# Graph network on one core: types counted by turn in the second permutation and in the pair counts, ranking by maximum, one register table, first gathers beside the table

## What is computed

```python
seg = concatenate([edge_type * n + src, (edge_type + R) * n + dst])   # R = 9, n = 3125
srcs = concatenate([dst, src])
# per layer: every node's row times 18 weight matrices; each edge takes the row of
# its far end and its type, scaled by factors of the counts of seg; sums by near end
deg = segment_sum(ones, dst, n)
```

## Time and profile before

| What | Value |
|---|---|
| Median of three runs | 5796.72 us |
| The profiled execution | 5791.65 us |
| Its span, first to last instruction | 5790.0 us |
| Busy: TensorE products, VectorE, GpSimd, ScalarE | 4358.3, 2903.5, 2059.3, 1183.2 us |
| Mean granted TensorE clock | 0.756 |
| First ranking and its permutation | about 15 to 411 us |
| Second ranking and its permutation | about 424 to 832 us |
| Staircase, pair counts | 874 to 896, 896 to 1325 us |
| Rgcn layer 0: table, sums | 3242 to 3340, 3345 to 4395 us |
| Rgcn layer 1: table, sums | 4420 to 4518, 4522 to about 5560 us |

### The profile page before, as it was taken

One profiled execution on the slowest core, in us unless ns is written; L12 is line 12 of the kernel. 1 busy time (PEld: TensorE's weight loads), 2 busy tenths in 40 slices (PEclk: granted clock), 3 DMA queues, 4 the chain that ended last, 5 costly groups with the idle time before them and its releaser, 6 DMA issues. The chain is left out here.

```text
span 5790.0 us, 73260 instructions
## 1 busy us (share of the span) xinstructions
PE 4358.3 (75%) x16465; PEld 2333.0 (40%) x16467; DVE 2903.5 (50%) x7206; ACT 1183.2 (20%) x3146; POOL 2059.3 (36%) x2143
## 2 busy tenths in 40 slices
PE   4985985557999996999978767767777666566658
PEld 1221221113655552454434355555553333343434
DVE  8999997761188886101152744433444422222233
ACT  3974973441400003111121100000000000000001
POOL 0000001110067760000000067777772577777730
PEclk9997996668999998999989855555557655555569
DMA  0000001225188881525514422222225322322233
GB/s 15 0 0 0 0 0 68 102 102 179 64 283 292 297 269 66 176 86 176 175 42 142 189 79 53 53 53 53 53 53 163 112 53 53 53 53 53 53 64 113
DMA packets 155477, 562.58 MB, mean 97 GB/s; under 512 B 42865, under 2 KB 51410, under 8 KB 155101
## 3 DMA queue, kind: packets, MB, share of 16 engines
q0 software_dynamic: 86816, 274.40, 16.9%
q1 hardware_dynamic: 68150, 286.11, 13.7%
q10 hardware_dynamic: 390, 0.60, 0.0%
HBM read 449.10 MB, written 111.85 MB: 97 GB/s over the span
## 5 line engine op out<-in xcount | busy, mean ns | idle before, releaser
L1850 PE MATMUL ps_sum_rgcn<-select_sum_rgcn,gathered_sum_rgcn 128*128 128x128 f32 x3328 | 1273.8, 492 | 564.4 <-DMA gathered_sum_rgcn<-by_dst,row 272.3
L1773 POOL DMA_INDIRECT gathered_sum_rgcn<-by_src,row x832 | 785.0, 944 | 1523.5 <-SPq L1734 1270.6
L1850 PEld LDWEIGHTS ps_sum_rgcn<-select_sum_rgcn,gathered_sum_rgcn 128*128 128x128 f32 x3328 | 839.3, 314 | 874.5 <-issue 866.6
L1773 POOL DMA_INDIRECT gathered_sum_rgcn<-by_dst,row x832 | 790.5, 950 | 253.5 <-issue 205.7
L608 PE MATMUL ps_sum_arma<-gathered_sum_arma,select_sum_arma 128*128 128x384 f32 x1664 | 554.0, 492 | 18.0 <-DMA gathered_sum_arma<-arma,other 15.4
L1459 PE MATMUL ps_sum_arma<-pair_counts_sum_arma,parts_sum_arma 128*128 128x512 f16 x2625 | 539.1, 361 | 14.2 <-DVE outT_arma_mid L1994 5.6
L594 POOL DMA_INDIRECT gathered_sum_arma<-arma,other x416 | 393.3, 945 | 435.7 <-POOLq L680 269.2
L1919 DVE TENSOR_TENSOR select_sum_rgcn<-one_hot_sum_rgcn,ps_coef_sum_rgcn 128x2048 f32<-128x2048 bf16 x52 | 118.9, 2287 | 769.1 <-PE ps_sum_rgcn L1850 769.1
L1880 ACT COPY sums_sum_rgcn<-ps_sum_rgcn 128x128 f32<-128x128 f32 x100 | 26.5, 265 | 2094.7 <-PE ps_sum_rgcn L1850 2094.7
L642 DVE TENSOR_TENSOR acc_arma_end<-acc_arma_end,ps_sum_arma 128x768 f32 x416 | 396.9, 954 | 57.1 <-PE ps_sum_arma L608 35.3
L608 PEld LDWEIGHTS ps_sum_arma<-gathered_sum_arma,select_sum_arma 128*128 128x128 f32 x1664 | 307.6, 190 | 264.2 <-issue 63.2
(11 more groups left out here) (385 smaller groups left out, 5765.2 us busy)
## 6 DMA issues: line engine op xcount, KB each, us to landing
pair_counts_sum_arma<-pairs SPq DMA_DIRECT2D x125, 800.0 KB, 4.3
by_src<-rows_rgcn_table SPq DMA_DIRECT2D x50, 576.0 KB, 2.8
by_dst<-rows_rgcn_table SPq DMA_DIRECT2D x50, 576.0 KB, 3.7
exact<-whole_pairs SPq DMA_DIRECT2D x25, 800.0 KB, 3.3
pairs<-half_pairs SPq DMA_DIRECT2D x25, 800.0 KB, 3.3
pair_counts_sum_x<-pairs SPq DMA_DIRECT2D x25, 800.0 KB, 4.4
pair_counts_sum_gcn<-pairs SPq DMA_DIRECT2D x25, 800.0 KB, 4.3
air_counts_sum_neighbour<-pairs SPq DMA_DIRECT2D x25, 800.0 KB, 4.3
```

The lines of the kernel that those rows point to most:

```text
L1773: nc.gpsimd.indirect_dma_start(got[:, n % PLACES, :], None, table, bass.IndirectOffsetOnAxis(ap=o.row[:, n % C:n % C + 1], axis=0)).then_i ...
L1850: nc.tensor.matmul(ps[:, bass.ds(ring[2 * v], P)], got[:, p, :], select[:, parity, u, :], start=False, stop=False, skip_group_check=True). ...
```

## The change

- `rank_stage`: TensorE sums the columns of all tiles so that a tile lies in a partition (`spot` picks the row). VectorE scans 400 (416) totals at once and computes a base per tile and column. For each of 25 blocks TensorE adds four products in PSUM (rank in the column, a large constant where the edge belongs to the tile, and the base in two bf16 parts), and VectorE takes the maximum over the blocks in two running buffers. ScalarE's copies of totals go.
- `Permute`: the group one-hot goes. High half and place come from one VectorE operation (compare, then multiply, with two scalars per partition); ScalarE makes the low half alone. Only the second permutation (by source, from the list by destination) counts, and it counts by destination: per turn of 16 columns VectorE makes type one-hots 9 wide, TensorE loads 16 group numbers of the chunks into registers and adds a product of nine columns at the group's place.
- Pair counts: the counts by source are made here, nine columns for each of the first 416 items, with type one-hots of all chunks made first. Four tables become two: TensorE loads one table of four values an item (place, column, free, group), VectorE one of two.
- Rgcn: the table stage is split in two of nine types (pieces of three, 384 columns). GpSimd's queue issues the first 32 gathers beside the second; the gathered buffer is now held by `rgcn_layer`.
- The second sort stands ahead of the degree stage; heavy and factor stages stand after the pair counts.

```diff
-            dve.wait_ge(kept, B + BLOCKS)
+            dve.wait_ge(totaled, 1)
+            then(nc.vector.tensor_copy(total[:, :], ps[0:NT, 0, 0:W]))
             then(nc.vector.tensor_tensor_scan(upto[:, :], total[:, :], total[:, :], 0.0, ALU.add, ALU.max))
...
+            for b in range(NT):
+                dve.wait_ge(filled_in, b + 1)
+                if b >= 2:
+                    dve.wait_ge(higher, b - 1)
+                nc.vector.tensor_tensor(best[e, b % 2, :], best[e, b % 2, :], ps[e, 3 + b % B, 0:W],
+                                        ALU.max).then_inc(higher, 1)
...
+                nc.tensor.matmul(place, triangle[0:ROWS, 0:ROWS], one_hot[0:ROWS, b, :], start=True, stop=False)
+                nc.tensor.matmul(place, big[0:ROWS, 0:ROWS], one_hot[0:ROWS, b, :], start=False, stop=False)
+                if b == 0:
+                    pe.wait_ge(shown, 1)
+                for part in (0, 1):
+                    last = nc.tensor.matmul(place, row_of[:, b, 0:ROWS], parts[:, part, :], start=False, stop=(part == 1))
+                last.then_inc(filled_in, 1)
...
+        if self.counts and u == 0:
+            dve.wait_ge(self.moved, i * U + self.V)
+            nc.vector.tensor_tensor(self.type[:, :, :], l.type[:, bass.ds(i * U, U), None].to_broadcast([P, U, R]),
+                                    k.iota[:, None, 0:R].to_broadcast([P, U, R]), ALU.is_equal).then_inc(self.typed, 1)
         dve.wait_ge(self.moved, n + 1)
         nc.vector.tensor_scalar(self.place[e, v, :], k.iota16[e, 0:P], o.slot_in[e, col], None,
                                 ALU.is_equal).then_inc(self.placed, 1)
-        nc.vector.tensor_scalar(self.chunk[e, v, :], k.iota16[e, 0:C], o.chunk_in[e, col], None, ALU.is_equal)
-        nc.vector.tensor_scalar(self.local[e, v, :], k.iota16[e, 0:P], o.local_in[e, col], None, ALU.is_equal)
-        nc.vector.tensor_scalar(self.group[e, v, :], k.iota16[e, 0:self.G], o.group_in[e, col], None,
+        nc.vector.tensor_scalar(self.slot[e, v, 0, :], k.iota16[e, 0:P], o.slot_in[e, col], o.high_in[e, col],
+                                ALU.is_equal, ALU.mult)
+        if self.counts:
+            nc.vector.tensor_scalar(self.local[e, v, :], k.iota16[e, 0:P], l.local[e, col], None, ALU.is_equal)
+        nc.vector.tensor_scalar(self.chunk[e, v, :], k.iota16[e, 0:C], o.chunk_in[e, col], None,
                                 ALU.is_equal).then_inc(self.column, 1)
...
+            nc.vector.tensor_tensor(type_hot[:, :, :], o.type[:, :, None].to_broadcast([P, C, R]),
+                                    k.iota[:, None, 0:R].to_broadcast([P, C, R]), ALU.is_equal)
...
-                places = load(PE, q.held_at, i * V, V, HELD - 1)
-                columns = load(PE, q.column_at, i * V, V, (SPANS - 1) * SPAN)
-                free = load(PE, q.free_at, i * V, V, BLOCKS_OF_PAIRS)
+                table = load(PE, q.item_at, i * (4 * V), 4 * V, (SPANS - 1) * SPAN)
                 for u in range(V):
-                    pe.wait_ge(freed, free[u])
+                    place, column, free, group = (
+                        nc.s_assert_within(x, low, top, skip_runtime_bounds_check_because="the staircase stays within its blocks")
+                        for x, low, top in zip(table[4 * u:4 * u + 4], (0, 0, 1, 0),
+                                               (HELD - 1, (SPANS - 1) * SPAN, BLOCKS_OF_PAIRS, G - R)))
                     pe.wait_ge(made, i * V + u + 1)
+                    if more:
+                        nc.tensor.matmul(ps_count[:, bass.ds(group, R)],
+                                         source[:, bass.ds(i * V + (u - base), 1), :].rearrange("p a f -> p (a f)"),
+                                         type_hot[:, bass.ds(i * V + u, 1), :].rearrange("p a r -> p (a r)"), start=False, stop=False, skip_group_check=True)
+                    pe.wait_ge(freed, free)
...
+                def gathers(gp):
+                    o = k.orders[0]
+                    for n in range(PLACES):
+                        nc.gpsimd.indirect_dma_start(
+                            got[:, n % PLACES, :], None, typed[0],
+                            bass.IndirectOffsetOnAxis(ap=o.row[:, n:n + 1], axis=0)).then_inc(k.arrived[n], 16)
...
-                table_stage(nc, k, f"rgcn_table{layer}", pieces,
-                            [(dram["by_src"], 0, R * D), (dram["by_dst"], R * D, R * D)], S2 * D)
+                table_stage(nc, k, f"rgcn_src_table{layer}", pieces(0), [(dram["by_src"], 0, R * D)], R * D)
+                table_stage(nc, k, f"rgcn_dst_table{layer}", pieces(R), [(dram["by_dst"], 0, R * D)], R * D,
+                            gathers=gathers)
```

270 lines of the change are left out of this document (146 added, 124 removed).

## The result

The kernel after takes 5825.19 us (median of five runs, 5822.57 to 5830.3) against 5795.31 of the kernel before; the ratio is 1.0053, 95% interval 1.0038 to 1.0067. It is slower, and the forecast was 5697 with a range of 5625 to 5785. The profiled execution has a span of 5820.9 us against 5790.0, so +30.9, where the sum said -99.5.

| Part | Before | After | Change | Forecast |
|---|---|---|---|---|
| First and second ranking | 92.1, 92.4 | 70.4, 71.3 | -43 | -86 |
| Permutation by destination | 313.8 | 262.0 | -52 | -68 |
| Permutation by source | 325.8 | 368.8 | +43 | +20 |
| Staircase | 21.4 | 23.0 | +2 | +1.5 |
| Pair counts | 425.1 | 544.3 | +119 | +68 |

A forecast was written before the change was run, and what follows sets the result against it. Stages between barriers, each bound by its slowest engine or queue: rankings -86, permutations -68 and +20, pair counts +68, staircase +1.5, rgcn -35, sum -99.5 us, giving 5697; range 5625 to 5785.

The forecast's parts named there:

- 0.67 us at 2.4 GHz, 17.3, plus 2 for a start at 1.2 GHz: First ranking: 25 blocks of four 400-column products at 0.67 us each, 17.3 us, plus 2 us for starting at low clock.
- My bound of -68: Both rankings: smallest gain, if blocks ran at 1.2 GHz throughout (1.35 us each) in one of the two; sum was -86.
- chose 0.17: Permutation by destination: new two-scalar operation takes 0.17 us, both pointers read together; 0.22 if read one after the other.
- Rival A: Permutations: the two-scalar compare is slow, 0.26 us, columns 0.67 and 0.82, whole 5770 us; chance 0.10.
- The pause: Permutation by source: at each of 26 turns VectorE waits for all products, some 1.05 us a turn, 27 us.
- the bound of +45: Permutation by source: largest loss, if the pauses bring TensorE to 1.2 GHz, 0.70 us a column; sum was +20.
- The count product was put at 0.18 us: Pair counts, first 52 turns: each item's nine-column count product takes 0.18 us to issue, bounds 0.03 and 0.34.
- the 2.8 us that GpSimd holds it are nearly covered now: 5 instead of 31: Pair counts: delays where GpSimd's conversion holds VectorE shrink to 5 us from 31, as longer turns cover them.
- Rival B: Pair counts: TensorE's queue pays an instruction per bounded value, 0.085 us each, +196 us, whole 5893 us; chance 0.08.
- Rival C: Pair counts: a table load costs 0.75 us whatever its size, stage -26 instead of +68, whole 5603 us; chance 0.09.
- The sum's own 0.12 a load: Pair counts: TensorE's table load priced at about 0.065 us a register and 0.12 a load, 2.9 us for the new table.
- fit under it: Rgcn: 32 gathers, 40 us, run beside the second table half, 49 us, without lengthening it; rgcn sum -35 us.

The follow-up runs named there:

- rank_rows: Kernel after, with both products that add the base run over 125 (128) rows instead of 25, added rows zero: 5778.82 us against 5784.45 of the kernel before.
- one_pointer: Kernel after plus one unused compare-and-multiply a column in both permutations, its second scalar a constant instead of a pointer: columns of 0.785 and 0.95 us, +0.16.

## Why the prediction was wrong

**Ranking, -43 instead of -86.** The chain ahead of the blocks took 6.2 us in the first ranking, where the sum had 7.9. The step that failed is "0.67 us at 2.4 GHz, 17.3, plus 2 for a start at 1.2 GHz": the low clock lasted all 25 blocks, and a block at that clock is not 1.35 but 1.71 us (1.61 in the second ranking). My bound of -68 let one of two rankings stay at 1.2 GHz and had no room for the second error. Of some 1.03 us a block, 0.67 is the clock (1.34 against 0.67) and 0.37 the mixture of 25 and 125 rows (rank_rows). The Trainium skill (TensorE: Matmul & The Clock Gate, Back-to-back issue gap) gives the gap at the low clock as the columns over 1.2 GHz, 0.333 us here; full rows agree to the hundredth (1.34 a block), the mixture doesn't (1.71).

**Permutation by destination, -52 instead of -68.** The mechanism and the bounds were right; I had computed 0.22 for the second pointer and chose 0.17. The trace's 0.06 for a pointer was the better guide than the thought that two are read together. 400 x 0.045 is 18 us, the whole miss of 16. Rival A, at 0.26, was too dear. The Trainium skill (VectorE: DVE Perf Modes, The perf-mode tier table) makes no exception for two pointers, and one_pointer bears it out for the elements; the 0.06 lies beside them.

**Permutation by source, +43 instead of +20.** The pause was right, 1.1 for 1.05. The same pointer is all of the miss: 416 x 0.057 is 24 us. That +43 lies within the bound of +45 is luck: the bound stood for TensorE at 1.2 GHz, and VectorE was what set the column.

**Pair counts, +119 instead of +68.** Two steps failed. The count product was put at 0.18 us, between a fixed one and a whole item; it costs 0.27, of which 0.02 is the product and 0.25 its three moving addresses. 52 turns of 0.5 us more are 26. And "the 2.8 us that GpSimd holds it are nearly covered now: 5 instead of 31" rested on a wrong reading of the earlier trace rows: the long turns were never VectorE's. They come from the stores, and stayed, some 31 us in all: 26 more. The one-hot that was ready 5.7 us early, in the trace of before, would have shown it. Rival B, the only one on the slower side, had the right place, TensorE's queue paying for register arithmetic, and the wrong operation: bounded values cost 0.01 us an item at most (turns of 5.48 us with four an item in the last 20, and of 5.40 before). Addresses are not free. Rival C was wrong: a load costs 0.25 and each register about 0.08. The sum's own 0.12 a load didn't follow from its rows, where the same 24 registers took 2.27 us in two loads and 2.7 in three; it came out near by a register priced too low. By the 200 ns a register of the Trainium skill (Runtime: NRT & Kernel Launch, Instruction fetch mechanics), which it gives for words in HBM, the eight more registers would have cost 115 us; the measured 0.08 for this table in SBUF says no, as the pause of before did.

**Rgcn, -36 for -35.** Right by its own steps on the chip of the result, on the second kind of chip not: the second half of the table 52 us with the gathers beside it, gather 32 at 3439.9 and 4594.1, 22.7 and 9.7 us after the sums begin (22 and 9 forecast). On the second kind the condition "fit under it" fails (83 to 85 us for 51), and nothing in the trace of before could have told; that the result came from the first kind is luck.

The range was too narrow for one reason above all: its parts were taken as independent, and the four misses share a source at least in part, a cost per operation that the sum took too low beside the data (pointers twice, addresses, kinds of weights). The long turns are a separate error.

## What to carry to other kernels

Before a product or a compare is added inside a loop, price its addresses and pointers, not its columns: a nine-column product with three register addresses cost 0.27 us an item against 0.02 with fixed ones. Where TensorE is to set the pace, give its products one row count, by zero rows if need be (1.71 us a block became 0.67), and put sums that share an operand into one product. A stall whose neighbour in the timeline looks guilty is to be checked by who had finished when: in the trace of before TensorE's first one-hot lay ready for 5.7 us, and that one line would have pointed away from VectorE. A name in the column of releasers is the signal that came last, not always the one that was waited for. And a transfer rate that fell is first to be multiplied by its stretch: 191 GB/s over 84 us and 277 over 51 are the same table, the gathers' 2 MB aside.

## What the hardware showed beside that

- TensorE, busy for all of 43 us, kept a granted clock of 0.50 (1.2 GHz) with half of its products on 25 rows; the same blocks with zeros added to full rows got 1.00 in both rankings, and over all runs it was 22 rankings of 22 against 8 of 8. The Trainium skill (TensorE: Matmul & The Clock Gate, What's actually happening) says that activity releases the throttle; the trace agrees for the full-row blocks and not for the mixture.
- The pause for a load of 32 registers into TensorE's queue grows from 2.4 us to about 3.65 with one store of 800 KB in it, and to 5.1 to 5.3 with two.
- Two kinds of chip differ where gathers run. On one TensorE uses a gathered chunk 3 us after its issue by the median, on the other 15 to 36, though the packets start as soon; the kernel before is 340 to 370 us longer there, and early gathers lose in place of gaining.
